# Transformer layer on one core: the next rows turned on VectorE and placed by DMA instead of turned on TensorE

## The chip, the cores and the metric

The kernel runs on one core of one Trainium2 chip. The metric is the device time of one execution in microseconds; lower is better. Before the change three timed runs took 1333.8 to 1335.08 us, with a median of 1334.93.

## The reference

One layer over `x` of 8 sequences x 2048 rows x 256 columns, all in float32:

```python
xn = (x - mean(x)) / sqrt(var(x) + 1e-5)              # layer norm of each row
q, k, v = split(xn @ wqkv); q = relu(q); k = relu(k)  # 16 heads of 16
kv = cumsum(k[..., :, None] * v[..., None, :])        # causal linear attention
attn = (q . kv) / (q . cumsum(k) + 1e-5) @ wo
sc = sigmoid(xn @ Wr); top2 = the two experts of 8 with the largest sc + router_bias
cw = sc at top2, divided by its sum + 1e-9; 0 elsewhere
routed = sum over e < 4 of cw[e] * (silu(xn @ Wg[e]) * (xn @ Wu[e])) @ Wd[e]
routed += (cw[4] + cw[6]) * xn + cw[7] * relu(xn)
shared = causal convolution of xn over 4 rows, per column, + conv_b
out = x + attn + routed + shared
```

Matrix products contract over the columns of `xn`, so TensorE needs `xn` with its columns on the partitions: `xT`. The convolution reads the same `xT`.

## The kernel before

The 16384 rows go in 32 batches of 512, four batches per sequence; `s` is the sequence, `j` the batch in it. A batch is T = 4 tiles of 128 rows. Every operand of a product is split into a high part in TensorE's fast float format and a low part (the rest), and a product is three passes: low x high, high x high, high x low (`product`, L299). For the rows of a batch the high part is `xh` (ScalarE, `high_x`, L530) and the low part `xl` = `xT` - `xh` (GpSimd, `low_x`, L665), each in two halves c = 0, 1 of 128 columns.

Each engine runs its own list of instructions in the order written; semaphores connect them. A batch has on TensorE:
1. for t = 0..3 `gate_up(t)` (expert t, 12 passes of 512 columns for gate, then up) and `numerators(t)` (small attention products of tile t, with the running state, `state_sum`);
2. after the numerators of t = 1, `turn_xn` for the next batch: eight 128 x 128 transposes by the identity into two PSUM banks (L307, called at L489);
3. `heads(s, j, 1)` (L326) for the next batch: values and router scores, then keys and queries. It begins with waits for both halves of `xh` and of `xl` of the next batch;
4. `output(t)` for t = 0..3, with the scores of the next batch ahead of t = 3.

The other engines, in the same batch:
- VectorE, per tile: state blocks (`blocks`), `gate_up` (the product `hid` of up and silu of gate, L836), `attend`, and a tap of the convolution (L828); then the statistics of the batch two ahead, `router`, `key_sums`, `products`, and the output adds, masks and inverses between them.
- ScalarE: silu, high parts, `fill_xT` (L518: copies the three rows of halo and the turned rows from PSUM into `xT`), `high_x` for both halves behind silu(2); then the evictions of `heads`, `same` and `relu` terms.
- GpSimd: `weigh(e)` (multiplies `hid` by the router's weight, L687; waits for VectorE's `hid` of that expert), `low_hid(e)` (L691), `low_y(t)` (L696), in the order weigh 0, low_y 0, weigh 1, low_hid 0, low_y 1, then `low_x` for c = 0 and 1 (L668), weigh 2, low_hid 1, low_y 2, weigh 3, low_hid 2, low_y 3, low_hid 3; then `base` (L671, waits for ScalarE's `same`) and `normalise` (L657, `xn` of the batch two ahead).
- SP: `spread_cw` (the router's weights to DRAM and back, broadcast to all partitions), the store of the batch's output, and the load of the batch four ahead.

`xT`, `xh`, `xl` and `xn` have two buffers each, chosen by the batch's parity.

Of the kernel before, what the change touches and what calls it, by code (L numbers as in the profile page):

```python
# [16 lines left out]
def layer_kernel(nc, x, wqkv, wo, w_router, router_bias, w_gate, w_up, w_down, conv_w, conv_b,  # L17
# [28 lines left out]
    with ExitStack() as ctx:  # L46
# [36 lines left out]
        rstd = sb("rstd", [P, T])  # L83
        xT = sb("xT", [P, 2, C, HALO + BT])
        xh, xl = sb("xh", [P, 2, C, BT], F32R), sb("xl", [P, 2, C, BT], F32R)
# [34 lines left out]
        hh, hl = sb("hh", [P, E, BT], F32R), sb("hl", [P, E, BT], F32R)  # L120
        cT = sb("cT", [P, C, BT])


# [49 lines left out]
        s_halo = sem("s_halo")  # L173
        s_xT = sem("s_xT")
        s_xh = sem("s_xh")
        s_xl = sem("s_xl")
# [47 lines left out]
        def chunk_at(s, j, n):  # L224


            return s * (CHUNKS - 1) + (2 * T * j + n if j < BPS else CHUNKS - 1 + n)

        def load_at(s, jk):

            return s * 16 + (jk // BPS + 1) * 16
# [12 lines left out]
        def _(sp):  # L244
# [15 lines left out]
            def spread_cw(s, j, k):  # L260
# [35 lines left out]
        def _(pe):  # L296
# [93 lines left out]
            def batch(s, j, left):  # L390
# [52 lines left out]
                def output(t):  # L443
# [35 lines left out]
                    else:  # L479
                        turn_conv()  # L480
                        add_attention()
                        add_hidden().then_inc(s_op, 1)

                for t in range(T):
                    gate_up(t)
                    numerators(t)
                    if t == 0:
                        scores(s, j, 0, 1)
                    if t == 1 and not last:  # L489
                        for c in range(C):  # L490
                            turn_xn(s, j, 1, c)
                if not last:
# [17 lines left out]
        def _(act):  # L510
# [6 lines left out]

            def fill_xT(s, j, k):  # L518
                p = (j + k) % 2

                if (j + k) % BPS:
                    act.activation(xT[:, p, :, 0:HALO], xT[:, 1 - p, :, BT:BT + HALO], ACT.Copy).then_inc(s_halo, 1)
                else:
                    act.activation(xT[:, p, :, 0:HALO], zeros[:, 0:C * HALO].rearrange("p (c h) -> p c h", c=C),
                                   ACT.Copy).then_inc(s_halo, 1)
                for c in range(C):
                    act.wait_ge(s_xtr, at(s, j, C, k * C + c + 1))
                    copy(xT[:, p, c, HALO:HALO + BT], XB[c][:, :]).then_inc(s_xT, 1)

            def high_x(s, j, k):  # L530
                p = (j + k) % 2
                for c in range(C):
                    act.wait_ge(s_xT, at(s, j, C, k * C + c + 1))
                    copy(xh[:, p, c, :], xT[:, p, c, HALO:HALO + BT]).then_inc(s_xh, 1)

# [35 lines left out]
            def batch(s, j, left):  # L571
# [16 lines left out]
                def first_tap():  # L588

                    act.wait_ge(s_out, at(s, j, T, T))  # L590
                    act.wait_ge(s_halo, at(s, j, 1, 1))
                    for c in range(C):
                        ins = act.activation(cT[:, c, :], xT[:, j % 2, c, 0:BT], ACT.Identity, bias=conv_bs[:, c:c + 1],
                                             scale=conv_ws[:, c, 0:1])
                    ins.then_inc(s_tap0, 1)
# [29 lines left out]
            for c in range(C):  # L625
# [4 lines left out]
            act.activation(sg[:, 0:1], zeros[:, 0:1], ACT.Sigmoid)  # L630
            act.activation(xT[:, 0, :, 0:HALO], zeros[:, 0:C * HALO].rearrange("p (c h) -> p c h", c=C),
                           ACT.Copy).then_inc(s_halo, 1)
# [15 lines left out]
        def _(pool):  # L648
# [16 lines left out]
            def low_x(s, j, k, c):  # L665
                p = (j + k) % 2
                pool.wait_ge(s_xh, at(s, j, C, k * C + c + 1))
                pool.tensor_tensor(xl[:, p, c, :], xT[:, p, c, HALO:HALO + BT], xh[:, p, c, :].bitcast(F32),  # L668
                                   ALU.subtract).then_inc(s_xl, 1)
# [10 lines left out]
            def batch(s, j, left):  # L680
# [23 lines left out]
                if not last:  # L704
                    for c in range(C):
# [12 lines left out]

# [7 lines left out]
        def _(dve):  # L726
# [24 lines left out]
            def router(s, j, k):  # L751
# [20 lines left out]
                dve.tensor_tensor(c46[:, :], cw[:, E, :], cw[:, E + 2, :], ALU.add).then_inc(s_cw, 1)  # L772

            def key_sums(s, j, k):
                for g in range(C):
# [43 lines left out]
            def batch(s, j, left):  # L819
                last = left == 0  # L820

                def tap(n):
# [4 lines left out]
                    for c in range(C):  # L827
                        ins = dve.scalar_tensor_tensor(out=cT[:, c, :], in0=xT[:, j % 2, c, n:n + BT],  # L828
                                                       scalar=conv_ws[:, c, n:n + 1], in1=cT[:, c, :],
# [69 lines left out]
            for c in (1, 0):  # L899
                dve.wait_ge(s_xtr, C)  # L900
                if c == 0:

                    dve.wait_ge(s_xh, 1)
                ins = dve.tensor_scalar(xT[:, 0, c, HALO:HALO + BT], XB[c][:, :], 1.0, None, ALU.mult)
                ins.then_inc(s_xT, 1)
            for c in range(C):
                dve.wait_ge(s_xT, C)
                dve.wait_ge(s_xh, c + 1)
                dve.tensor_tensor(xl[:, 0, c, :], xT[:, 0, c, HALO:HALO + BT], xh[:, 0, c, :].bitcast(F32),
                                  ALU.subtract).then_inc(s_xl, 1)  # L910
# [62 lines left out]
```

## Time and profile before

| | |
|---|---|
| timed runs | 1333.8, 1334.93, 1335.08 us |
| the profiled execution's own time | 1334.1 us |
| its span, first to last instruction | 1332.3 us |
| TensorE busy (matmul) | 1312.0 us, 98% |
| VectorE busy | 1120.6 us, 84% |
| GpSimd busy | 822.7 us, 62% |
| ScalarE busy | 737.4 us, 55% |
| TensorE's granted clock | 9 tenths or more in all 40 slices of the span, mean 0.997 |
| DMA | 73.73 MB in 46828 packets, mean 55 GB/s |

Busy time is the sum of an engine's instructions, whatever they wait for; it does not tell which engine sets the time. The chain of waits does: it goes back from the last instruction and names at each step what released it. A timeline lists the instructions of one engine in order of time, with the idle time in front of an instruction and what ended it in brackets. Matmuls are pipelined: their listed durations overlap, so what one costs is the distance between starts. Times are in us unless marked ns.

### The profile page before, as it was taken

The page shows a single profiled execution, that of the slowest core. Times are in us where ns is not written, and L with a number is a line of the kernel's source. Part 1 is how long each engine was busy: PE and PEld are TensorE (multiplying, and loading weights), DVE is VectorE, ACT ScalarE, POOL GpSimd, SP SyncE. Part 2 cuts the span into 40 slices and gives each one's busy share as a digit, 9 for nine tenths or more (in the row PEclk, how much of TensorE's full clock was granted, in tenths as well). Part 3 has the DMA queues.
Part 4 walks back from the last instruction along what each step waited for, and adds up shares of the span by engine and source line. Part 5 has one row for each costly group of instructions (what it writes and reads, how often), then busy time and mean ns, then how long its engine had stood idle before and what let it go on. Part 6 is the DMA issues. An engine that isn't in the chain of part 4 may idle for free.

```text
span 1332.3 us, 54753 instructions
## 1 busy us (share of the span) xinstructions
PE 1312.0 (98%) x24384; PEld 1136.9 (85%) x24384; DVE 1120.6 (84%) x2574; ACT 737.4 (55%) x1543; POOL 822.7 (62%) x673
## 2 busy tenths in 40 slices
PE   5999999999999999999999999999999999999998
PEld 4888888888888888888888888888888888888887
DVE  7988889888898888898888988888888889888885
ACT  5645566545556455565555564556645655545561
POOL 2676566675575755666656757556666566575554
PEclk9999999999999999999999999999999999999999
DMA  5011211111211111111111011111111111111110
GB/s 181 30 39 66 66 53 47 35 66 66 66 34 50 51 66 65 50 50 35 66 66 65 35 49 51 66 66 50 50 34 67 66 65 35 35 65 50 51 49 18
DMA packets 46828, 73.73 MB, mean 55 GB/s; under 512 B 6529, under 2 KB 42241, under 8 KB 42497
## 3 DMA queue, kind: packets, MB, share of 16 engines
q1 hardware_dynamic: 45888, 69.23, 15.2%
q8 instruction: 191, 3.13, 1.0%
q10 hardware_dynamic: 704, 1.01, 0.2%
q14 instruction: 45, 0.36, 0.1%
HBM read 53.18 MB, written 17.04 MB: 53 GB/s over the span
## 4 chain that ended last, share of the span: by engine, by line
PE 97%; DVE 1%; POOL 0%; ACT 0%; DMA 0%; issue 0%; POOLq 0%; DVEq 0%
PE ring L303 51%; PE scores L303 17%; PE ring L423 7%; PE ring L439 6%; PE scores L372 5%; PE state_sum L386 4%; PE ring L459 2%; PE scores L312 2%; PE scores L354 2%; DMA x_t<-in_L_attn_x_dram 0%; DVE cT L828 0%; ACT qp L548 0%; DVE sm L807 0%; PE scores L321 0%; POOL hid L687 0%
## 5 line engine op out<-in xcount | busy, mean ns | idle before, releaser
L687 POOL TENSOR_TENSOR hid<-hid,cwb 128x512 f32<-128x512 f32 x128 | 172.0, 1343 | 225.4 <-DVE hid L836 224.7
L828 DVE SCALAR_TENSOR_TENSOR cT<-xT,conv_ws,cT 128x512 f32<-128x512 f32 x192 | 292.3, 1561 | 0.0
L675 POOL TENSOR_TENSOR x_t<-x_t,same 128x1024 f32<-128x1024 f32 x32 | 76.9, 2404 | 242.7 <-ACT same L557 242.7
L814 DVE TENSOR_TENSOR state_bd<-state_sum,tables_s 128x256 f32<-128x256 f32 x248 | 103.7, 418 | 135.9 <-PE state_sum L386 135.8
L578 ACT ACTIVATE sg<-ring 128x512 f32<-128x512 f32 x128 | 76.8, 600 | 251.3 <-PE ring L303 251.3
L303 PE MATMUL ring<-xl,wgu_h 128*128 128x512 f32 x512 | 212.3, 415 | 0.0
L691 POOL TENSOR_TENSOR hl<-hid,hh 128x512 fp32r<-128x512 f32 x128 | 208.4, 1628 | 0.0
L303 PE MATMUL ring<-xh,wgu_l 128*128 128x512 f32 x512 | 203.0, 396 | 0.0
L303 PE MATMUL ring<-xh,wgu_h 128*128 128x512 f32 x512 | 202.2, 395 | 0.0
L511 ACT ACTIVATE yh<-yT 128x256 fp32r<-128x256 f32 x128 | 53.5, 418 | 246.5 <-DVE yT L845 246.5
L807 DVE TENSOR_TENSOR sm<-scores,causal_s 128x512 f32<-128x512 f32 x256 | 158.5, 679 | 21.6 <-PE scores L372 21.6
L303 PE MATMUL ring<-wd_l,hh 128*128 128x256 f32 x512 | 143.5, 280 | 3.4 <-DVE yT L845 2.1
L303 PE MATMUL ring<-wd_h,hl 128*128 128x256 f32 x512 | 143.5, 280 | 0.0
L303 PE MATMUL ring<-wd_h,hh 128*128 128x256 f32 x512 | 143.3, 280 | 0.0
L696 POOL TENSOR_TENSOR yl<-yT,yh 128x256 fp32r<-128x256 f32 x128 | 129.9, 1015 | 0.0
L423 PE MATMUL ring<-sm,vp 64*32 64x64 f32 x8192 | 118.8, 225 | 0.0
L303 PEld LDWEIGHTS ring<-xl,wgu_h 128*128 128x128 f32 x512 | 96.7, 189 | 24.7 <-issue 5.5
L303 PEld LDWEIGHTS ring<-xh,wgu_l 128*128 128x128 f32 x512 | 96.5, 189 | 22.6
L303 PEld LDWEIGHTS ring<-xh,wgu_h 128*128 128x128 f32 x512 | 97.2, 190 | 17.5
L386 PEld LDWEIGHTS state_sum<-vp,ktok 64*32 64x32 f32 x3968 | 54.0, 107 | 55.0 <-issue 49.5
L423 PEld LDWEIGHTS ring<-sm,vp 64*32 64x32 f32 x8192 | 98.1, 105 | 2.9 <-issue 2.9
L303 PE MATMUL scores<-xh,wqk_l 128*128 128x512 f32 x256 | 100.1, 391 | 0.0
(118 smaller groups left out, 3528.1 us busy)
## 6 DMA issues: line engine op xcount, KB each, us to landing
cwb<-cw_rows SPq DMA_DIRECT2D x32, 1024.0 KB, 4.7
x_t<-in_L_attn_x_dram SPq DMA_DIRECT2D x32, 512.0 KB, 4.4
out_dram<-x_t SPq DMA_DIRECT2D x31, 512.0 KB, 2.9
cw_rows<-cwt SPq DMA_DIRECT2D x128, 2.0 KB, 1.4
sm<-in_L_attn_wqkv_dram ACTq DMA_DIRECT2D x2, 384.0 KB, 5.0
sm<-in_L_ffn_Wg_dram SPq DMA_DIRECT2D x2, 256.0 KB, 3.5
sm<-in_L_ffn_Wu_dram SPq DMA_DIRECT2D x2, 256.0 KB, 4.6
cwb<-in_L_ffn_Wd_dram SPq DMA_DIRECT2D x1, 512.0 KB, 5.7
```

Of the source, the lines that this page charges most:

```text
L303: ins = mm(dst, lhs, rhs, start=first and n == 0, stop=final and n == len(passes) - 1, skip_group_check=not (first and final))
L386: ins = mm(ST[rows, g, :], ktok[toks, t, g, rows], vp[toks, t, g * PPG + m, 0:3:2, :], start=first and g == 0, stop=True, skip_group_check ...
L423: mm(NB2[t % 2][h][BLK * m:BLK * m + BLK, gs], window, sm[toks, t // 2, t % 2, 2 * pair + par, :], start=par == 0 and g == 0, stop=False, ...
L439: ins = mm(NB2[t % 2][h][rows, g * HALF:(g + 1) * HALF], state_bd[:, n % 4, cols], qT[:, g, n0:n0 + HALF], start=False, stop=True, skip_gr ...
L578: act.activation(sg[:, :], GB[t % 2], ACT.Silu).then_inc(s_sg, 1)
L675: pool.tensor_tensor(xb, xb, same[:, :, :], ALU.add).then_inc(s_base1, 1)
L687: pool.tensor_tensor(hid[:, e, :], hid[:, e, :], cwb[:, e, :], ALU.mult).then_inc(s_hid, 1)
L691: pool.tensor_tensor(hl[:, e, :], hid[:, e, :], hh[:, e, :].bitcast(F32), ALU.subtract).then_inc(s_hl, 1)
L696: pool.tensor_tensor(yl[:, :, t * P:(t + 1) * P], yT[:, t % 2, :, :], yh[:, :, t * P:(t + 1) * P].bitcast(F32), ALU.subtract).then_inc(s_y ...
L807: dve.tensor_tensor(heads, SB[f][:, :].rearrange("p (t a n) -> p t a n", a=2, n=HALF), causal2_s[:, :].unsqueeze(1).unsqueeze(1).to_broadc ...
L814: dve.tensor_tensor(state_bd[:, n % 4, :].rearrange("p (g m n) -> p g m n", g=C, m=PPG), ST.unsqueeze(2).to_broadcast([P, C, PPG, BLK]), s ...
L828: ins = dve.scalar_tensor_tensor(out=cT[:, c, :], in0=xT[:, j % 2, c, n:n + BT], scalar=conv_ws[:, c, n:n + 1], in1=cT[:, c, :], op0=ALU.m ...
```

## The change

In every batch but the first, `xn` of the batch after next is turned in the output stage of the current batch. VectorE turns it in blocks of 32 x 32 (`turn_x`, four instructions, between `router` and `key_sums`) into a new buffer `xb_t`; SP then issues 32 transfers (`place_turned`), each of which moves one row and one column of blocks of one half to its place in `xT`. TensorE's `turn_xn` stays for batch 1 alone, and so do ScalarE's copies out of PSUM. `normalise` goes ahead of `base` on GpSimd. `high_x` and `low_x` take one half per call, and the second half of each has a new place: on ScalarE behind silu(3), on GpSimd behind `weigh(3)`. `heads` takes over one of the waits of `turn_xn`. In front of `gate_up(0)` of each batch but the last TensorE gets 32 waits for a semaphore that was met at the start. `xT` has 32 columns of lead in place of 3 and another address.

```diff
+    LEAD = 32
+    QUADS = P // 32
+    FILL = 32
+        xT = sb("xT", [P, 2, C, LEAD + BT])
+        xb_t = sb("xb_t", [P, C, QUADS, T, BLK])
+            def place_turned(s, j, k):
+                sp.wait_ge(s_turn, at(s, j, 1, k - 1))
+                for c in range(C):
+                    for a in range(QUADS):
+                        for q in range(QUADS):
+                            row = xT[q * BLK:(q + 1) * BLK, (j + k) % 2, c, LEAD:LEAD + BT]
+                            sp.dma_start(row.rearrange("p (t a n) -> p t a n", t=T, a=QUADS)[:, :, a, :],
+                                         xb_t[a * BLK:(a + 1) * BLK, c, q, :, :]).then_inc(xT_in[c], 16)
...
                 if left:
                     spread_cw(s, j, 1)
+                if left > 1:
+                    place_turned(s, j, 2)
...
             def heads(s, j, k):
                 p = (j + k) % 2
+                if k:
+                    pe.wait_ge(s_sm, at(s, j, U * ROWS, U * ROWS))
                 pe.wait_ge(s_xh, at(s, j, C, k * C + C))
                 pe.wait_ge(s_xl, at(s, j, C, k * C + C))
...
+                if not last:
+                    for _ in range(FILL):
+                        pe.wait_ge(tables_in, 16)
                 for t in range(T):
                     gate_up(t)
                     numerators(t)
                     if t == 0:
                         scores(s, j, 0, 1)
-                    if t == 1 and not last:
+                    if s == j == 0 and t == 1:
                         for c in range(C):
-                            turn_xn(s, j, 1, c)
+                            turn_xn(0, 0, 1, c)
...
                 high_y(1)
                 if not last:
-                    fill_xT(s, j, 1)
+                    lead(s, j, 1)
                 silu(2)
                 if not last:
-                    high_x(s, j, 1)
+                    high_x(s, j, 1, 0)
                 high_hid(1)
                 high_y(2)
                 silu(3)
+                if not last:
+                    high_x(s, j, 1, 1)
...
                 low_y(1)
                 if not last:
-                    for c in range(C):
-                        low_x(s, j, 1, c)
+                    low_x(s, j, 1, 0)
                 weigh(2)
                 low_hid(1)
                 low_y(2)
                 weigh(3)
+                if not last:
+                    low_x(s, j, 1, 1)
                 low_hid(2)
                 low_y(3)
                 low_hid(3)
+                if left > 1:
+                    normalise(s, j, 2)
                 if not last:
                     base(s, j, 1)
-                if left > 1:
-                    normalise(s, j, 2)
...
+            def turn_x(s, j, k):
+                dve.wait_ge(s_xn, at(s, j, 1, k + 1))
+                if s + j:
+                    for c in range(C):
+                        dve.wait_ge(xT_in[c], turned_at(s, j, k - 1))
+                for t in range(T):
+                    ins = dve.transpose(xb_t[:, :, :, t, :], xn[:, (j + k) % 2, t, :]
+                                        .rearrange("p (c q n) -> p c q n", c=C, q=QUADS))
+                ins.then_inc(s_turn, 1)
...
                     router(s, j, 1)
+                    if left > 1:
+                        turn_x(s, j, 2)
                     key_sums(s, j, 1)
```

## Rows read from the trace of the kernel before

**Rows 1.** The chain that ended last, by engine (page, part 4).
```profile
PE 97%; DVE 1%; POOL 0%; ACT 0%; DMA 0%; issue 0%; POOLq 0%; DVEq 0%
```

**Rows 2.** Timeline of TensorE: start, us, line, operation, out<-in, count.
```profile
653.25 1.09 PE L312 MATMUL scores<-tables_s,xn 128*128 128x128 f32 x8
654.10 0.47 PE L303 MATMUL ring<-xl,wgu_h 128*128 128x512 f32 x1
```

**Rows 3.** Timeline of GpSimd in two batches.
```profile
657.09 2.14 POOL L668 TENSOR_TENSOR xl<-xT,xh 128x512 fp32r<-128x512 f32 x2
...
663.41 1.29 POOL L687 TENSOR_TENSOR hid<-hid,cwb 128x512 f32<-128x512 f32 x1
664.66 1.74 POOL L691 TENSOR_TENSOR hl<-hid,hh 128x512 fp32r<-128x512 f32 x1
...
667.50 1.30 POOL L691 TENSOR_TENSOR hl<-hid,hh 128x512 fp32r<-128x512 f32 x1
676.59 2.40 POOL L675 TENSOR_TENSOR x_t<-x_t,same 128x1024 f32<-128x1024 f32 x1 [7.78 <-ACT same L557]
...
745.11 1.29 POOL L687 TENSOR_TENSOR hid<-hid,cwb 128x512 f32<-128x512 f32 x1 [0.42 <-DVE hid L836]
```

**Rows 4.** Timeline of TensorE, first product of `heads` in the same two batches.
```profile
663.22 0.39 PE L303 MATMUL scores<-wvr_l,xh 128*128 128x264 f32 x1
...
744.71 0.39 PE L303 MATMUL scores<-wvr_l,xh 128*128 128x264 f32 x1
```

**Rows 5.** Timeline of VectorE in the first of these batches.
```profile
646.04 0.42 DVE L814 TENSOR_TENSOR state_bd<-state_sum,tables_s 128x256 f32<-128x256 f32 x1 [2.43 <-PE state_sum L386]
...
662.65 0.68 DVE L836 TENSOR_TENSOR hid<-ring,sg 128x512 f32<-128x512 f32 x1
```

**Rows 6.** Timeline of TensorE near the span's start and end, after idle times.
```profile
27.83 1.20 PE L372 MATMUL scores<-qp,kT 32*64 32x128 f32 x64 [2.32 <-ACT ktok L511]
...
30.30 0.63 PE L303 MATMUL ring<-xh,wgu_l 128*128 128x512 f32 x1
30.73 0.63 PE L303 MATMUL ring<-xl,wgu_h 128*128 128x512 f32 x1
...
32.93 0.39 PE L303 MATMUL ring<-xl,wgu_h 128*128 128x512 f32 x1
33.16 0.39 PE L303 MATMUL ring<-xh,wgu_h 128*128 128x512 f32 x1
...
1316.89 0.39 PE L303 MATMUL ring<-wd_l,hh 128*128 128x256 f32 x1 [2.13 <-DVE yT L845]
...
1319.62 0.58 PE L303 MATMUL ring<-wd_l,hh 128*128 128x256 f32 x1 [1.30 <-POOL hl L691]
```

**Rows 7.** Windows: stretch, length, busy by engine, granted clock, DMA share, GB/s.
```profile
29.00:31.00 2.00, 2.00 (x22) 1.65 (x21) 1.97 (x4) 1.55 (x2) 1.65 (x1) 0.52 0.90 369
31.00:33.00 2.00, 2.00 (x7) 1.52 (x7) 2.00 (x4) 0.76 (x3) 0.73 (x1) 0.63 0.26 98
...
1320.00:1322.00 2.00, 2.00 (x11) 2.00 (x11) 0.00 (x0) 0.00 (x0) 0.00 (x0) 0.50 0.00 0
```

**Rows 8.** VectorE groups by shape: busy us, mean ns, idle before in us.
```profile
L789 DVE STREAM_TRANSPOSE qks_tok<-qks 128x512 f32<-128x512 f32 x64 | 41.8, 691 | 1.1
...
L771 DVE STREAM_TRANSPOSE cwt<-cw 128x32 f32<-128x32 f32 x32 | 6.8, 212 | 1.1
...
L764 DVE TENSOR_TENSOR hot<-hot 128x32 f32<-128x32 f32 x32 | 6.3, 197 | 1.1
```

**Rows 9.** Timeline of SP's transfers: start, us to issue, line, out<-in, count.
```profile
672.06 1.71 SPq L265 DMA_DIRECT2D cw_rows<-cwt  x4
674.77 0.34 SPq L272 DMA_DIRECT2D cwb<-cw_rows  x1
```

**Rows 10.** DMA issues (page, part 6): count, KB each, median us to landing.
```profile
cw_rows<-cwt SPq DMA_DIRECT2D x128, 2.0 KB, 1.4
```

**Rows 11.** Timeline of ScalarE, `silu(3)` of the batch after the first of rows 3.
```profile
701.05 0.60 ACT L578 ACTIVATE sg<-ring 128x512 f32<-128x512 f32 x1 [0.70 <-PE ring L303]
```

More of the change, by code:

```diff
@@ L83, in layer_kernel @@
         rstd = sb("rstd", [P, T])
-        xT = sb("xT", [P, 2, C, HALO + BT])
+        xT_gap = sb("xT_gap", [P, 12])
         xh, xl = sb("xh", [P, 2, C, BT], F32R), sb("xl", [P, 2, C, BT], F32R)
@@ L121, in layer_kernel @@
         cT = sb("cT", [P, C, BT])
+        xT_room = sb("xT_room", [P, 8])
+        xT = sb("xT", [P, 2, C, LEAD + BT])
+        xb_t = sb("xb_t", [P, C, QUADS, T, BLK])
         rdT = qks
@@ L174, in layer_kernel @@
         s_xT = sem("s_xT")
+        s_turn = sem("s_turn")
+        xT_in = [sem(f"xT_in{c}") for c in range(C)]
         s_xh = sem("s_xh")
@@ L227, in chunk_at, with turned_at @@
             return s * (CHUNKS - 1) + (2 * T * j + n if j < BPS else CHUNKS - 1 + n)
+        def turned_at(s, j, k):
+            return (s * BPS + j + k - 1) * (16 * QUADS * QUADS)
         def load_at(s, jk):
@@ L516, in high_weights, with lead, high_x @@
                     copy(hi, src).then_inc(w_hi, 1)
-            def fill_xT(s, j, k):
+            def lead(s, j, k):
                 p = (j + k) % 2
                 if (j + k) % BPS:
-                    act.activation(xT[:, p, :, 0:HALO], xT[:, 1 - p, :, BT:BT + HALO], ACT.Copy).then_inc(s_halo, 1)
+                    act.activation(xT[:, p, :, LEAD - HALO:LEAD], xT[:, 1 - p, :, LEAD + BT - HALO:LEAD + BT],
+                                   ACT.Copy).then_inc(s_halo, 1)
                 else:
-                    act.activation(xT[:, p, :, 0:HALO], zeros[:, 0:C * HALO].rearrange("p (c h) -> p c h", c=C),
+                    act.activation(xT[:, p, :, LEAD - HALO:LEAD], zeros[:, 0:C * HALO].rearrange("p (c h) -> p c h", c=C),
                                    ACT.Copy).then_inc(s_halo, 1)
-                for c in range(C):
-                    act.wait_ge(s_xtr, at(s, j, C, k * C + c + 1))
-                    copy(xT[:, p, c, HALO:HALO + BT], XB[c][:, :]).then_inc(s_xT, 1)
-            def high_x(s, j, k):
-                p = (j + k) % 2
-                for c in range(C):
-                    act.wait_ge(s_xT, at(s, j, C, k * C + c + 1))
-                    copy(xh[:, p, c, :], xT[:, p, c, HALO:HALO + BT]).then_inc(s_xh, 1)
+                if s + j == 0:
+                    for c in range(C):
+                        act.wait_ge(s_xtr, C + c + 1)
+                        copy(xT[:, p, c, LEAD:LEAD + BT], XB[c][:, :]).then_inc(s_xT, 1)
+            def high_x(s, j, k, c):
+                p = (j + k) % 2
+                if s + j:
+                    act.wait_ge(xT_in[c], turned_at(s, j, k))
+                else:
+                    act.wait_ge(s_xT, C + c + 1)
+                copy(xh[:, p, c, :], xT[:, p, c, LEAD:LEAD + BT]).then_inc(s_xh, 1)
             def heads(s, j, k):
@@ L592, in first_tap @@
                     for c in range(C):
-                        ins = act.activation(cT[:, c, :], xT[:, j % 2, c, 0:BT], ACT.Identity, bias=conv_bs[:, c:c + 1],
+                        ins = act.activation(cT[:, c, :], xT[:, j % 2, c, LEAD - HALO:LEAD - HALO + BT], ACT.Identity, bias=conv_bs[:, c:c + 1],
                                              scale=conv_ws[:, c, 0:1])
@@ L630, in _ @@
             act.activation(sg[:, 0:1], zeros[:, 0:1], ACT.Sigmoid)
-            act.activation(xT[:, 0, :, 0:HALO], zeros[:, 0:C * HALO].rearrange("p (c h) -> p c h", c=C),
+            act.activation(xT[:, 0, :, LEAD - HALO:LEAD], zeros[:, 0:C * HALO].rearrange("p (c h) -> p c h", c=C),
                            ACT.Copy).then_inc(s_halo, 1)
@@ L667, in low_x @@
                 pool.wait_ge(s_xh, at(s, j, C, k * C + c + 1))
-                pool.tensor_tensor(xl[:, p, c, :], xT[:, p, c, HALO:HALO + BT], xh[:, p, c, :].bitcast(F32),
+                pool.tensor_tensor(xl[:, p, c, :], xT[:, p, c, LEAD:LEAD + BT], xh[:, p, c, :].bitcast(F32),
                                    ALU.subtract).then_inc(s_xl, 1)
@@ L704, in batch @@
                 if not last:
-                    for c in range(C):
-                        low_x(s, j, 1, c)
+                    low_x(s, j, 1, 0)
                 weigh(2)
@@ L772, in router @@
                 dve.tensor_tensor(c46[:, :], cw[:, E, :], cw[:, E + 2, :], ALU.add).then_inc(s_cw, 1)
+            def turn_x(s, j, k):
+                dve.wait_ge(s_xn, at(s, j, 1, k + 1))
+                if s + j:
+                    for c in range(C):
+                        dve.wait_ge(xT_in[c], turned_at(s, j, k - 1))
[3 more added lines that the diff above has]
+                ins.then_inc(s_turn, 1)
             def key_sums(s, j, k):
@@ L827, in tap @@
                     for c in range(C):
-                        ins = dve.scalar_tensor_tensor(out=cT[:, c, :], in0=xT[:, j % 2, c, n:n + BT],
+                        ins = dve.scalar_tensor_tensor(out=cT[:, c, :], in0=xT[:, j % 2, c, LEAD - HALO + n:LEAD - HALO + n + BT],
                                                        scalar=conv_ws[:, c, n:n + 1], in1=cT[:, c, :],
@@ L903, in _ @@
                     dve.wait_ge(s_xh, 1)
-                ins = dve.tensor_scalar(xT[:, 0, c, HALO:HALO + BT], XB[c][:, :], 1.0, None, ALU.mult)
+                ins = dve.tensor_scalar(xT[:, 0, c, LEAD:LEAD + BT], XB[c][:, :], 1.0, None, ALU.mult)
                 ins.then_inc(s_xT, 1)
@@ L908, in _ @@
                 dve.wait_ge(s_xh, c + 1)
-                dve.tensor_tensor(xl[:, 0, c, :], xT[:, 0, c, HALO:HALO + BT], xh[:, 0, c, :].bitcast(F32),
+                dve.tensor_tensor(xl[:, 0, c, :], xT[:, 0, c, LEAD:LEAD + BT], xh[:, 0, c, :].bitcast(F32),
                                   ALU.subtract).then_inc(s_xl, 1)
```

## Prediction

> **What bounds the kernel now.** I read the chain of waits first: TensorE holds 97% of it [rows 1], so TensorE's own work sets the time, and another engine counts only where TensorE has to wait for it. The span of 1332.3 us holds 32 batches of one pattern, some 41 us each, so a stage can be read from one batch. Then I read the timeline of each engine over that batch, looking for two things: what TensorE no longer does, and which wait would now end last in front of it.
>
> **The transposes that go.** Eight transposes start at 653.25 and the next product at 654.10 [rows 2], so they cost TensorE 0.85 us. They stand in every batch but the last, 31 times, and the change keeps them in the first, so 30 x 0.85 = 25.5 us come off. With them go ScalarE's two copies out of PSUM per batch; ScalarE is busy for 55% of the span, so these give nothing.
>
> **The wait that comes.** The diff also moves work that its title does not name. Before, both halves of the low part (`low_x`, c = 0 and 1) ran on GpSimd ahead of `weigh(2)`: they start at 657.09 and take 2.14 us [rows 3], and TensorE's `heads` starts at 663.22 [rows 4], four microseconds later. After, `low_x(1)` stands behind `weigh(3)` in GpSimd's queue. `weigh(3)` waits for `hid` of tile 3, which VectorE makes from the last gate and up product; and `heads` waits for both halves in its first lines, before it does anything. So a chain VectorE `hid` - GpSimd `weigh(3)` - GpSimd `low_x(1)` - TensorE `heads` is formed, and on TensorE only `numerators(3)` lies beside it.
>
> Its length, against the moment at which `heads` could start (663.22 and 744.71 in two batches [rows 4]):
> - VectorE's `hid` of tile 3 starts at 662.65 and takes 0.68 [rows 5], so it ends 0.11 after that moment, and `weigh(3)` follows at 663.41, 0.19 after it; in the other batch `weigh(3)` starts at 745.11 [rows 3], 0.40 after it. I take 0.2 (0 to 0.4), the nearer of the two, since GpSimd has one operation less before it. The 0.85 us does not shorten this: VectorE, which waits for TensorE's state sum in every tile, moves up with TensorE.
> - `weigh(3)` holds GpSimd from 663.41 to 664.66 [rows 3]: 1.25.
> - `low_x(1)`: 1.07 each in the pair of before. Here it runs beside VectorE's convolution taps, where `hl`, an operation of the same shape, takes 1.74 instead of 1.30 [rows 3]. 1.07 x 1.74 / 1.30 = 1.43 (1.07 to 1.74).
> - GpSimd's end to TensorE's first product: 0.15 (0.05 to 0.2), as an estimate from the 0.08 between the end of VectorE's `hid` and `weigh(3)` and a first weight load that is no longer done ahead.
>
> Sum 0.2 + 1.25 + 1.43 + 0.15 = 3.0 us of an idle TensorE in each of 31 batches (2.4 to 3.5): 93 us. It does not come back: before, TensorE had nothing to wait for that this idle time could hide.
>
> **The clock.** TensorE stood for 2.32 us before 27.83, and for 2.13 and 1.30 us before 1316.89 and 1319.62 [rows 6]. After the first of these the granted clock reads 0.52 and 0.63, after the others 0.50 [rows 7]: the lower level, 1.2 GHz instead of 2.4, for some 3.4 us each time. At that level a product of 512 columns comes every 0.43 us (30.30 to 30.73), at the upper level every 0.23 (32.93 to 33.16) [rows 6]. Eight fit in 3.4 us, so a low stretch costs 8 x 0.20 = 1.6 us; I take 1.55, because the narrower products of `heads` lose a little less. Both places in the running kernel where TensorE stood over 2 us were followed by one, and a gap of 3 us is longer than either. I take 28 of 31: 28 x 1.55 = 43 us (0 to 48).
>
> **What is added on VectorE.** Four 32 by 32 block transposes of 128 x 256, between `router` and `key_sums`. The trace has them at 128 x 32 (212 ns) and 128 x 512 (691 ns) [rows 8]; four cost 0.85 to 2.8 us, by their place between the two about 1.5. Behind them on VectorE wait key sums, products, output adds and masks, for which TensorE waits at the start of the next batch. There VectorE sits idle for 2.43 us, waiting for TensorE [rows 5]; with the new wait in front of `heads` it also gets to `router` before its scores are there. So nothing; without that cover it would be up to 31 x 2.8 = 87 us. `normalise` is moved ahead of `base` on GpSimd, which stands idle there for 7.78 us until ScalarE delivers `same` [rows 3], so into that idle time; should the transposes have to wait a little for it, the same 2.43 us cover that.
>
> **What is added on SP.** 32 transfers per batch, behind the spread of the router's weights and ahead of the output store. Four small ones take 1.71 us to issue [rows 9], 0.43 each: 13.7 us from about 675.1 (674.77 + 0.34 [rows 9]), and a small one lands 1.4 us later [rows 10], so all lie by 690. The second half is wanted after `silu(3)` of the next batch, 701.05 + 0.5 [rows 11]. That leaves over 11 us, so nothing; the store and the next load go out some 5 us later, with more than a batch to spare. This holds until a transfer takes over 0.78 us ((701.55 - 675.1 - 1.4) / 32).
>
> The transfers move runs of 128 bytes. The Trainium skill (DMA: Bandwidth & Descriptors, Specifications) says that below 512 bytes the engines do a read-modify-write; its section on why small descriptors are slow limits the penalty to HBM. By the second the sum stays as it is; by the first the landing grows, and only past the 0.78 us does time move. No row shows 4096 such runs in one batch.
>
> **The 32 waits in front of `gate_up`.** All have long been met. A wait that VectorE puts between two of its operations leaves it idle for 1.1 us in 32 times, 34 ns each [rows 8], the time of the signal included. So 32 cost at most 1.1 us a batch, 34 us in all; below nothing is excluded, since they do no work. Nothing if TensorE's queue holds enough work: the output products just ahead take 1.4 us per tile. I take nothing. The Trainium skill (TensorE: Matmul & The Clock Gate, on engine queue depths) gives TensorE a queue of 64; by it the sum has 0 here, by the row alone up to 34 us more.
>
> **The sum.** On the profiled execution (1334.1 us, span 1332.3; the three timed runs have a median of 1334.93, 0.06% above): 1334.1 - 25.5 + 93 + 43 = 1444.6 us, say 1445: slower by 8%.
>
> **Rivals.**
> 1. *The stall without the clock.* The gap falls so that the clock stays up. For it: in the running batches the granted clock was never low. Against it: [rows 6, 7]. 1334.1 - 25.5 + 93 = 1402 us.
> 2. *The chain is hidden; faster.* `low_x(1)` is done before `numerators(3)` ends, TensorE keeps its 0.85 us. For it: GpSimd is busy 62% of the span only, and the data comes a batch ahead. Against it: `weigh(3)` alone ends 1.4 us after `heads` is due [rows 3, 4]. It decides where the stall is under 0.82 us a batch (25.5 / 31); without any, 1334.1 - 25.5 = 1309 us.
> 3. *The transfers come late.* Their runs are short and there are 4096 of them in a batch. If each transfer took 1 us, 675.1 + 32 + 1.4 = 708.5 against 701.55 would add 7 us in each of 30 batches: 1445 + 210 = 1655 us. Against it: the room of 11 us.
> 4. *The 32 waits are in the open*: 1445 + 34 = 1479 us.
>
> **How the numbers follow.** Forecast 0.63, its own range 1420 to 1465 (28 falls, 2.4 to 3.5 us of stall give 1427 to 1460). Rival 1 0.23 (1384 to 1418), rival 2 0.06, rival 3 0.04, rival 4 0.04. The range 1388 to 1472 holds the forecast and nearly all of rival 1. Faster by over 0.2% needs rival 2: 0.05; within 0.2% (what a measurement of this kernel can tell from no change) its edge, where the stall just eats the gain: 0.01; slower 0.94.
>
> **What would show it.** TensorE idle in front of the first product of `heads` for about 3 us, 31 times, released by GpSimd's `xl`; `xl` of c = 1 starting right behind `weigh(3)`; the granted clock at 0.5 for a few microseconds in most batches, TensorE's busy share near 92%; no transposes of `xn` but the first; block transposes of some 0.43 us; `place_turned` over before the output store; no idle time in front of `gate_up(0)`. The prediction is wrong if `heads` starts without a gap, and 43 us too high if the clock stays up.

## The result, and the profile after

The changed kernel takes 1476.26 us (1471.71 to 1479.86 in four runs) where the kernel before takes 1334.91: ratio 1.1058, 95% interval 1.1045 to 1.1071. It was forecast at 1445 in a range up to 1472. The direction and the chain of causes came as forecast; the sum was 31 us too small, and the time lies above the top of the stated range. The profiled execution takes 1474.79 us, with a span of 1473.0 and a mean granted clock of 0.955 (0.997 before).

The page of the changed kernel, parts 1 and 4 (it answers to [rows 1]):

```profile
PE 1342.3 (91%) x24144; PEld 1164.6 (79%) x24144; DVE 1215.5 (83%) x2694; ACT 715.3 (49%) x1483; POOL 827.9 (56%) x673
...
PE 81%; DVE 10%; POOL 7%; issue 2%; ACT 0%; DMA 0%; POOLq 0%; DVEq 0%
```

VectorE and GpSimd, which had 1% of the chain between them, now have 17%. The view of waits of TensorE (who waits for whom; us in total, times, longest) says where:

```profile
PE scores L330 <- POOL xl L710: 102.9, 31, 3.4
...
PE scores L402 <- issue: 5.4, 7, 0.9
...
PE ring L330 <- issue: 2.1, 2, 1.4
```

One large new wait, 31 times, 3.32 us each: the first product of `heads` waits for GpSimd's `low_x`. The chain that ended last shows one of these gaps piece by piece (start, us, what):

```profile
726.80 0.69 DVE hid L891
727.49 0.07 issue
727.55 1.27 POOL hid L729
728.82 1.68 POOL xl L710
730.50 0.14 issue
730.63 2.98 PE scores L330 x12
```

This is VectorE `hid` - GpSimd `weigh(3)` - GpSimd `low_x(1)` - TensorE `heads`. On GpSimd's own timeline the two halves of `low_x` were back to back in [rows 3]; here they stand apart, and the second one is longer:

```profile
722.10 1.28 POOL L710 TENSOR_TENSOR xl<-xT,xh 128x512 fp32r<-128x512 f32 x1
...
728.77 1.71 POOL L710 TENSOR_TENSOR xl<-xT,xh 128x512 fp32r<-128x512 f32 x1
```

TensorE over the same stretch (it answers to [rows 2], [rows 4] and [rows 6]):

```profile
717.65 0.69 PE L469 MATMUL ring<-qT,state_bd 128*64 128x64 f32 x16
718.26 0.50 PE L330 MATMUL ring<-xl,wgu_h 128*128 128x512 f32 x1
...
726.75 0.69 PE L469 MATMUL ring<-qT,state_bd 128*64 128x64 f32 x16
730.63 0.56 PE L330 MATMUL scores<-wvr_l,xh 128*128 128x264 f32 x1 [3.20 <-POOL xl L710]
730.99 0.42 PE L330 MATMUL scores<-wvr_h,xh 128*128 128x264 f32 x1
731.21 0.42 PE L330 MATMUL scores<-wvr_h,xl 128*128 128x264 f32 x1
...
736.05 0.63 PE L330 MATMUL scores<-xl,wqk_h 128*128 128x512 f32 x1
736.48 0.54 PE L330 MATMUL scores<-xh,wqk_h 128*128 128x512 f32 x1
736.86 0.40 PE L330 MATMUL scores<-xh,wqk_l 128*128 128x512 f32 x1
737.09 0.39 PE L330 MATMUL scores<-xl,wqk_h 128*128 128x512 f32 x1
...
741.63 0.39 PE L330 MATMUL scores<-xh,wqk_l 128*128 128x512 f32 x1
```

The kernel before has, ahead of the transposes of [rows 2] and at the end of the `heads` of [rows 4]:

```profile
652.64 0.69 PE L439 MATMUL ring<-qT,state_bd 128*64 128x64 f32 x16
...
671.48 0.39 PE L303 MATMUL scores<-xh,wqk_l 128*128 128x512 f32 x1
```

Behind the gap a product of 264 columns starts every 0.22 us, where the trace of the kernel before has 0.12, and the 512-column products come 0.43 apart until 736.48, then 0.23 (736.86 to 737.09): the lower clock level lasts some 6 us of this `heads`. From its first to its last product it takes 11.00 us (730.63 to 741.63), before the change 8.26 (663.22 to 671.48). The windows say it directly (stretch, length, busy us by engine with counts for TensorE, weight load, VectorE, ScalarE, GpSimd, then granted clock, DMA share, GB/s; it answers to [rows 7]):

```profile
728.00:731.40 3.40, 0.77 (x3) 0.80 (x4) 3.40 (x4) 0.99 (x2) 3.40 (x3) 0.79 0.22 71
732.00:735.40 3.40, 3.40 (x18) 3.40 (x17) 2.06 (x9) 2.62 (x7) 3.19 (x5) 0.50 0.00 0
736.00:739.40 3.40, 3.40 (x16) 2.81 (x15) 2.34 (x21) 1.11 (x4) 1.50 (x3) 0.88 0.00 0
```

This batch is one of the slower ones. Windows of 12 us, each from about the start of a gap, show three kinds of batches:

```profile
189.00:201.00 12.00, 8.84 (x58) 7.71 (x55) 11.11 (x44) 6.45 (x16) 10.02 (x11) 1.00 0.01 4
592.00:604.00 12.00, 8.64 (x69) 7.89 (x56) 9.92 (x38) 5.14 (x13) 10.37 (x11) 0.86 0.15 45
727.00:739.00 12.00, 8.80 (x52) 8.18 (x48) 9.05 (x34) 4.74 (x12) 10.20 (x11) 0.72 0.14 43
```

Of the 31 gaps, 2 read 1.00 (the clock did not fall), 22 read 0.86 and 7 read 0.72. Since the lower level is half the upper one, 0.86 means some 3.4 us of 12 at the lower level, and 0.72 twice that. The `heads` behind them take 8.24 us, 9.70 and 10.92 in the mean. Summed over the 31 batches they take 306.2 us, against 256.4 before the change: 49.9 us more.

VectorE's idle time and new transposes, and SP's transfers (answering to [rows 5, 8, 9]):

```profile
736.77 0.22 DVE L797 TENSOR_TENSOR scoreb<-score,bias_s 128x32 f32<-128x32 f32 x1 [2.64 <-ACT score L580]
...
739.90 1.42 DVE L825 STREAM_TRANSPOSE xb_t<-xn 128x256 f32<-128x256 f32 x4
```

```profile
698.96 22.82 SPq L297 DMA_DIRECT2D xT<-xb_t  x32
```

The transposes cost what was estimated (411 ns each in the mean over 120). The placing takes 0.71 us a transfer in this batch, not 0.43, and still ends in time: no wait of ScalarE for it stands in this trace.

In front of `gate_up(0)` the changed kernel has idle time once, in the first batch:

```profile
30.63 0.77 PE L330 MATMUL ring<-xl,wgu_h 128*128 128x512 f32 x1 [1.44 <-issue]
```

**The sum of the parts.** 1332.3 - 25.5 (transposes) + 102.9 (the gap) + 49.9 (`heads` behind it, the clock) + 7.5 (idle on "issue", none of it before) = 1467.1, for a span of 1473.0. The 5.9 us that are left are busy time of TensorE outside these `heads`: 1342.3, against 1312.0 - 25.5 + 49.9 = 1336.4. Their cause stays open. As much stands in experiments 7 and 10, where the clock stays up behind the gaps.

### The profile page after: what moved, and what is told of

Read it like the earlier page. It is cut to its first block, busy times and chain, and to the rows that moved or that the text cites. A ratio compares the mean times of both kernels' runs of the same rounds, so it can differ in the third digit from the quotient of the medians.

```text
span 1473.0 us, 55758 instructions
## 1 busy us (share of the span) xinstructions
PE 1342.3 (91%) x24144; PEld 1164.6 (79%) x24144; DVE 1215.5 (83%) x2694; ACT 715.3 (49%) x1483; POOL 827.9 (56%) x673
## 4 chain that ended last, share of the span: by engine, by line
PE 81%; DVE 10%; POOL 7%; issue 2%; ACT 0%; DMA 0%; POOLq 0%; DVEq 0%
PE ring L330 42%; PE scores L330 18%; DVE cT L883 6%; PE scores L402 5%; PE ring L453 5%; PE ring L469 4%; POOL xl L710 4%; PE state_sum L416 3%; POOL hid L729 3%; PE ring L489 2%; PE scores L384 2%; DVE hid L891 1%; DVE yT L900 1%; DVE state_bd L869 1%; DMA x_t<-in_L_attn_x_dram 0%
## 5 line engine op out<-in xcount | busy, mean ns | idle before, releaser
L729 POOL TENSOR_TENSOR hid<-hid,cwb 128x512 f32<-128x512 f32 x128 | 164.0, 1281 | 339.8 <-DVE hid L891 339.0
L883 DVE SCALAR_TENSOR_TENSOR cT<-xT,conv_ws,cT 128x512 f32<-128x512 f32 x192 | 302.5, 1614 | 0.0
L330 PE MATMUL scores<-wvr_l,xh 128*128 128x264 f32 x128 | 53.2, 416 | 105.7 <-POOL xl L710 102.9
L330 PEld LDWEIGHTS scores<-wvr_l,xh 128*128 128x128 f32 x128 | 36.2, 283 | 109.4 <-issue 109.4
L738 POOL TENSOR_TENSOR yl<-yT,yh 128x256 fp32r<-128x256 f32 x128 | 122.3, 956 | 0.0
L330 PEld LDWEIGHTS ring<-xh,wgu_l 128*128 128x128 f32 x512 | 96.5, 188 | 22.8 <-issue 0.2
L330 PE MATMUL scores<-xl,wqk_h 128*128 128x512 f32 x256 | 101.9, 398 | 0.0
```

Of the source, the lines that this page charges most:

```text
L330: ins = mm(dst, lhs, rhs, start=first and n == 0, stop=final and n == len(passes) - 1, skip_group_check=not (first and final))
L729: pool.tensor_tensor(hid[:, e, :], hid[:, e, :], cwb[:, e, :], ALU.mult).then_inc(s_hid, 1)
L738: pool.tensor_tensor(yl[:, :, t * P:(t + 1) * P], yT[:, t % 2, :, :], yh[:, :, t * P:(t + 1) * P].bitcast(F32), ALU.subtract).then_inc(s_y ...
```

## The experiments

All times are medians, each set against runs of the kernel before on the same chip (1334.1 to 1335.5). Where an experiment stands on another, its diff is against that one.

**1. The order undone, the change kept.** Both halves of the next batch are split and subtracted together again, ahead of `weigh(2)`.

```diff
 # ScalarE
                     high_x(s, j, 1, 0)
+                    high_x(s, j, 1, 1)
...
                 silu(3)
-                if not last:
-                    high_x(s, j, 1, 1)
 # GpSimd
                     low_x(s, j, 1, 0)
+                    low_x(s, j, 1, 1)
                 weigh(2)
...
                 weigh(3)
-                if not last:
-                    low_x(s, j, 1, 1)
```

> The change with the second halves back where they stood: high_x(1) right behind high_x(0), low_x(1) right behind low_x(0), both ahead of weigh(2). Theory A (the loss is the wait of heads for low_x(1), 3.3 us in 31 batches, and the low clock that follows it): both go, the 25.5 us of the transposes stay off, so 1305 to 1320 us, no idle time of TensorE in front of heads, mean granted clock back at 0.99 or more. Theory B (the loss is the added work: the short transfers, VectorE's transposes, the 32 waits): little changes, 1440 to 1480 us.

Measured: 1517.06 us, 1.1374 [1.1355, 1.1393]; both theories missed it. The wait of `heads` is gone, as theory A said, but another took its place, and it is larger:

```profile
PE ring L489 <- DVE x_t L938: 128.5, 30, 4.4
```

The timelines of VectorE, GpSimd and TensorE show why:

```profile
713.03 1.42 DVE L823 STREAM_TRANSPOSE xb_t<-xn 128x256 f32<-128x256 f32 x4
...
716.83 5.47 DVE L839 TENSOR_TENSOR qks<-qT,ksum 128x512 f32<-128x512 f32 x2
...
724.87 0.74 DVE L938 TENSOR_TENSOR x_t<-ring,x_t 128x256 f32<-128x256 f32 x2
...
716.38 2.61 POOL L716 TENSOR_TENSOR x_t<-x_t,same 128x1024 f32<-128x1024 f32 x1 [3.38 <-ACT same L597]
719.07 2.68 POOL L719 TENSOR_TENSOR x_t<-x_t,xn 128x1024 f32<-128x1024 f32 x1
...
725.34 0.69 PE L489 MATMUL ring<-tables_s,cT 128*128 128x128 f32 x2 [4.40 <-DVE x_t L938]
```

VectorE's two `products` (two SBUF inputs) take 5.47 us instead of 1.29. The first is due at 716.83, when GpSimd's `base` has run since 716.38; the pair ends at 722.30, 0.55 behind the end of `base` (721.75). Before, the pair ended at 675.60 and `base` began at 676.59 [rows 3]. The new transposes push the products back by 1.4 us, and a tiny operation beside GpSimd's `hl`, `vare`, takes another 1.1 (1.29 for 0.16 before). The first output add waits behind them, and TensorE for that. In the changed kernel the two do not meet: there the pair is over at 744.87, and `base` begins at 746.73, when ScalarE's `same` is done. That it is the gap which holds `same` back so long was not tried by itself.

**2. The order alone, without the change.** The kernel before, with only the second half moved as the change moves it (`high_x` takes the half as an argument here, too; that edit is left out below).

```diff
-                    high_x(s, j, 1)
+                    high_x(s, j, 1, 0)
 # ScalarE, behind silu(3)
+                if not last:
+                    high_x(s, j, 1, 1)
 # GpSimd
-                    for c in range(C):
-                        low_x(s, j, 1, c)
+                    low_x(s, j, 1, 0)
 # GpSimd, behind weigh(3)
+                if not last:
+                    low_x(s, j, 1, 1)
```

> The kernel before with one part of the change alone: the second halves moved, high_x(1) behind silu(3), low_x(1) behind weigh(3); the transposes stay on TensorE, nothing is added on SP or VectorE. Theory A: 1335 + 31 x 3.3 + some 57 for the clock = 1495 us (1480 to 1505), slower than the whole change by its 25.5 us less what the change adds elsewhere. Theory B: 1335 us, as before.

Measured: 1477.96 us, 1.1071 [1.1053, 1.1090]: the whole loss, with the transposes still on TensorE and no new transfer, and 2 us below the range of theory A, since the gaps are 2.82 us each and not 3.3.

```profile
PE scores L303 <- POOL xl L670: 87.4, 31, 3.0
```

1332.3 + 87.4 + 60.0 (TensorE's busy time, 1372.0 against 1312.0) = 1479.7, for a span of 1479.4. All 31 gaps are followed by a low stretch. No idle time on "issue" stands in this trace.

**3. TensorE kept busy in the gap.** The changed kernel with 13 products into a buffer that `heads` overwrites, ahead of its two waits.

```diff
 # TensorE, heads, ahead of its waits for the split halves
+                    for _ in range(13):
+                        mm(SB[0][:, :], wqk_h[:, 0, 0:P], xh[:, 1 - p, 0, :], start=True, stop=True)
```

> The change with 13 products of 512 columns put in front of the two waits at the head of heads, into a PSUM bank that is free there and is written over afterwards; they fill about 3.0 of the 3.3 us in which TensorE stands. They leave the stall as long as it is. Theory A: the clock stays at its upper level and its share comes off, some 57 us of 1476: 1410 to 1430 us, mean granted clock 0.99. If the clock were no part of the loss: 1476 us or a little more.

Measured: 1436.89 us, 1.0770 [1.0752, 1.0788], clock 0.995: 39 us faster for 403 products of work that nobody needs.

```profile
PE scores L404 <- issue: 13.5, 16, 1.4
...
PE scores L330 <- POOL xl L712: 5.8, 23, 0.3
```

The 31 `heads` take 255.3 us again, for 306.2 in the changed kernel. So the clock's term is a consequence of the gap. It missed the expected 1410 to 1430 by 7 us; the idles on "issue" doubled (13.5 + 1.6 = 15.1 against 7.5).

**4. Without the 32 met waits** in front of `gate_up` (`FILL = 0`).

```diff
-    FILL = 32
+    FILL = 0
```

> The change without the 32 met waits in front of gate_up(0). Theory A: they cost nothing, 1470 to 1480 us. If they are in the open at up to 34 ns each: 31 x 1.1 = 34 us come off, 1442 us.

Measured: 1478.11 us (1471.65 to 1481.09), against the change's 1471.71 to 1479.86: no difference that these runs can tell. One place does differ. The first `gate_up(0)`, which in the changed kernel starts behind 1.44 us of idle time, starts here without any:

```profile
29.98 0.79 PE L330 MATMUL ring<-xl,wgu_h 128*128 128x512 f32 x1
```

**5. The collision taken out.** Experiment 1, with `base` of the next batch held until the denominators are summed.

```diff
             def base(s, j, k):
+                if k:
+                    pool.wait_ge(s_den, at(s, j, 1, k + 1))
```

> This is the early order (both halves of the next batch split before the second weighting) with one wait more: GpSimd's 'base' of the next batch waits until VectorE's denominators are summed. Theory A (the 128.5 us in which TensorE waited for the first output add came from one collision: VectorE's two-input product, 0.69 us apart from GpSimd and 2.6 us beside GpSimd's two-input 'base'): the mean of the product falls from 2623 ns to 0.7, the wait of L489 for x_t from 128.5 us to under 30 (the add then ends about 0.3 us behind TensorE: 30 x 0.3 = 9), the clock goes above 0.98, and the time is 1315 to 1340. Theory B (VectorE's chain is late by the transposes themselves, 1.3 us, and by the statistics' 1.1 us, base or not): products still 0.7 us but a wait of over 1 us in each batch, and the time 1380 to 1480. If the placing on SP (22.8 us, ended at 739) is now late, ScalarE shows a wait for it before the split, under 4 us in each batch.

Measured: 1401.67 us, 1.0505 [1.0488, 1.0523], 115 us faster than experiment 1. The products are back at their old time, and TensorE's wait for the add is 0.7 us in all (group of VectorE: busy, mean ns):

```profile
L841 DVE TENSOR_TENSOR qks<-qT,ksum 128x512 f32<-128x512 f32 x64 | 41.4, 688 | 1.1
```

The collision was the cause of that wait. The time is still not that of theory A: with TensorE faster the placing comes late, as the last sentence of the expectation allowed for.

```profile
ACT xh L547 <- DMA xT<-xb_t: 123.9, 30, 6.8
```

```profile
PE state_sum L416 <- ACT sg L618: 30.1, 20, 3.5
```

ScalarE stands 4.1 us a batch in front of the second half, a little over the 4 that were allowed for, and its silu behind that is late for TensorE.

**6. The same without the 32 waits** (`FILL = 0`).

> The run before without the 32 met waits in front of the turned batch's products. Theory A (the met waits cost nothing even where TensorE is not held up by anything else): the same time within 3 us. Theory B (they were hidden only by the stall): 5 to 34 us faster.

Measured: 1404.45 us (1400.63 to 1406.89) against 1397.6 to 1405.22: no difference, here too. The 1.44 us ahead of the first `gate_up(0)` stand in experiment 5 and are gone in this one.

**7. The second half one place later.** Experiment 5, with the split behind `silu(3)` and the subtraction between `low_y(2)` and `weigh(3)`.

```diff
 # ScalarE
-                    high_x(s, j, 1, 1)
...
                 silu(3)
+                if not last:
+                    high_x(s, j, 1, 1)
 # GpSimd
-                    low_x(s, j, 1, 1)
...
                 low_y(2)
+                if not last:
+                    low_x(s, j, 1, 1)
                 weigh(3)
```

> As the first of these, but the second half is split behind the last silu and subtracted between GpSimd's third low_y and its last weighting, so that the placing has some 5 us more. Theory A (only what stands on GpSimd between the half's turn and heads counts, and here nothing does): the same as the first within 10 us, and no wait for the placing. Theory B (the subtraction, 1.3 to 1.7 us, now delays the last weighting and so TensorE's last sums): a wait of 0.5 to 1.5 us in each batch at ring for hl or hid, 15 to 60 us more than the first with its clock.

Measured: 1361.55 us, 1.0201 [1.0184, 1.0218]. The placing is in time again, but `low_x(1)` delays `weigh(3)`, ends 1.2 us after `heads` is due, and a smaller gap is back, 1.27 us each; the clock stays up (0.995).

```profile
PE scores L330 <- POOL xl L710: 39.5, 31, 1.6
```

Neither theory had it whole: the wait is B's in size, but it stands at `heads`, not at the sums.

**8. The transposes behind the first two output adds.** Experiment 7, with VectorE's `turn_x` moved.

```diff
-                    if left > 1:
-                        turn_x(s, j, 2)
                     key_sums(s, j, 1)
...
                 for t in range(T):
+                    if t == 2 and left > 1:
+                        turn_x(s, j, 2)
```

> As the third of these, but VectorE turns the rows behind its first two output adds, not ahead of the key sums: the four transposes are then off the chain products, denominators, first add. Theory A (that chain is what the transposes were in the way of): the wait of L489 for x_t goes to nearly nothing, the placing starts some 4 us later and is still there for the second half; time 1305 to 1320. Theory B (the place on VectorE does not matter once base is held back): the same as the third within 3 us. Theory C (the placing now comes late for the first half): ScalarE waits at the split and the time goes up by 20 us or more.

Measured: 1498.00 us, 1.1217 [1.1199, 1.1236]: theory C. SP's placing starts 5 us behind the weights' rows and runs into the split.

```profile
710.93 0.34 SPq L287 DMA_DIRECT2D cwb<-cw_rows  x1
716.25 24.42 SPq L297 DMA_DIRECT2D xT<-xb_t  x32
```

```profile
ACT xh L547 <- DMA xT<-xb_t: 122.4, 30, 5.3
```

```profile
PE scores L330 <- POOL xl L710: 119.1, 31, 5.1
```

**9. Two queues for the placing.** Experiment 5, with two transfers ahead of the wait for the weights' rows and the last four on ScalarE's queue, behind the denominators. The lines below are the main ones; `place` issues the transfers from one number up to another.

```diff
+        EARLY, SPLIT = 2, 28
 # SP, behind the four transfers of the weights' rows
+                    place(sp, s, j, 2, 0, EARLY)
 # SP, place_turned: 26 of the 32
+                place(sp, s, j, k, EARLY, SPLIT)
 # ScalarE, behind denominators
+                    place(act, s, j, 2, SPLIT, 32)
```

> The early order with base held back, in which ScalarE waited 123.9 us in all (30 times, about 4.1) for the placing, which took SP 23.8 us. Here two of the 32 transfers go out while the weights' rows are still on their way, and the last four from ScalarE's queue behind the denominators; everything else is the same. Theory A (the whole loss left, 66 us, is the late placing: 6 x 0.72 = 4.3 us sooner leaves nothing of it): ScalarE's wait for the placing under 20 us, no wait of TensorE for sg, and 1310 to 1330. Theory B (the transfers cost what their descriptors cost, on whichever queue: the queue is not the limit, or ScalarE's own issues hold its silu up by 2.9 us): the placing still ends after 22 us or the silu is late, and the time is within 15 us of 1401.

Measured: 1336.67 us (1331.76 to 1346.87), 1.0024 [1.0003, 1.0045]: 65 us faster than experiment 5 and level with the kernel before. ScalarE's wait for the placing is 13.2 us in all (123.9 there), TensorE's wait for `sg` 0.3. Theory A named the cause; its 1310 to 1330 missed by 7 us.

**10. The second half once more later.** Experiment 9, split behind `high_y(2)`, subtracted behind `low_hid(1)`.

```diff
 # ScalarE
                 high_y(2)
+                if not last:
+                    high_x(s, j, 1, 1)
 # GpSimd
                 low_hid(1)
+                if not last:
+                    low_x(s, j, 1, 1)
                 low_y(2)
```

> As the one before, but the second half is split behind ScalarE's third high_y and subtracted behind GpSimd's second low_hid, still ahead of the last weighting by one low_y: a few us more for the placing. Theory A: nothing waits for the placing any more, the half is subtracted before the last weighting, so heads does not wait either: 1308 to 1325, faster than before by 1 to 2%. Theory B (GpSimd has no room for 1.3 to 1.7 us anywhere in the last 20 us ahead of heads): heads waits 1 us or more in each batch as when the subtraction stood one step later (39.5 us), and the time is 1350 to 1365.

Measured: 1339.35 us, 1.0035 [1.0021, 1.0049], between the ranges of both theories. `heads` waits again, 0.6 us each:

```profile
PE scores L336 <- POOL xl L718: 17.9, 30, 0.7
```

**11. That subtraction one step up**, ahead of `low_hid(1)`.

```diff
+                if not last:
+                    low_x(s, j, 1, 1)
                 low_hid(1)
-                if not last:
-                    low_x(s, j, 1, 1)
```

> As the one before, in which the second half's subtraction ended 0.5 us too late for heads (17.9 us in all), but with that subtraction one step up on GpSimd, behind its third weighting and ahead of its second low_hid (1.7 us sooner); nothing else. Theory A (the 17.9 us and the idles they bring are all that is left of the loss): no wait of TensorE for xl, and 1312 to 1325, 1 to 1.5% faster than before. Theory B (GpSimd's work as a whole is what is late, and the wait only moves to the sums that low_hid feeds): a wait for hl of some 0.5 us in each batch, 1330 to 1345. Theory C (something that no named wait shows, as the idles on issue and the tenth of a batch that differs between runs of the two-queue kernels): no named wait and still 1328 to 1340.

Measured: 1336.22 us (1333.61 to 1341.54), 1.0022 [1.0010, 1.0034]: theory C. No wait of TensorE for `xl` is left, and no gain:

```profile
PE ring L495 <- DVE x_t L950: 4.7, 22, 0.2
...
PE scores L408 <- issue: 5.3, 4, 1.6
...
PE ring L336 <- issue: 2.7, 3, 1.4
...
PE state_sum L422 <- DVE x_t L950: 1.1, 7, 0.2
```

Its span, 1334.4, is 1332.3 - 25.5 + 17.3 more idle time of TensorE + 10.3 more busy time. Of the 17.3, 8.0 are on "issue" and 5.8 wait for the output add, a fifth of a microsecond at a time; the rest is smaller still. Of the 10.3 a part is the clock (0.995 against 0.997); the rest stays open, and with it why 25.5 us less of transposes leave no gain.

## Why the prediction fell short

**What is missing.** On the profiled execution the sum said 1444.6, and 1474.8 came. The 30.2 us are 9.9 of the gap, 6.9 of the clock, 7.5 of idle time on "issue" and 5.9 of other busy time. All four lie on the same side.

**The transposes that go: right.** With them the next `gate_up` starts 1.46 us behind the product in front of them (652.64 to 654.10), without them 0.61 (717.65 to 718.26): 0.85 us, 30 times. TensorE's busy time does not fall by all of it. In experiments 7 and 10, where the clock stays up, it is 1292.3 and 1292.1, 20 us below the 1312.0 of before and not 25.5.

**The wait that comes: right in mechanism, 10 us too small; the largest miss.** It was forecast as 0.2 + 1.25 + 1.43 + 0.15 = 3.0 us. The chain shown above reads 0.12 (from the end of TensorE's work, 727.43, to 727.55) + 1.27 + 1.68 + 0.13; in the mean of the 31 batches the four terms are 0.24 + 1.22 + 1.71 + 0.15 = 3.32. The term that was mis-sized is `low_x(1)`: 1.71 us, for which the forecast took 1.43. It scaled the time of the old place, 1.07, by what the taps do to `hl`. Its own upper row, 1.74, was of an operation of the same shape at the very place where this one was moved, beside VectorE's taps; that row would have been the price. Experiment 2 shows that the order alone makes the gap, and experiment 1 that it goes with the order.

**The clock: right that it falls, 7 us too small.** The step that failed is "for some 3.4 us each time", taken as the length of every low stretch. The clock fell behind 29 of the 31 gaps, where the forecast took 28, and a low stretch of that length cost `heads` 1.43 us, where it took 1.55. But 7 of the 29 lasted twice as long and cost 2.65 us each. Together that is 49.9 us for 43. The few low stretches of before, all at its ends, were no sample of what follows a gap in the running kernel; the upper end of the forecast's bound, 48 us, fell with the same assumption. The prediction's "both places" left one out, too: in the kernel before TensorE also stood for 2.80 us ahead of 13.67, and the granted clock from 13.00 to 20.00 is 1.00.

**Idle time on "issue": not foreseen, 7.5 us.** 1.4 us of it belong to the 32 waits (see below). The rest, 3 to 14 us, stands in every kernel that has the placing and in neither kernel that lacks it (before, and experiment 2). That the many short transfers cause it is argued from this alone and was not tried by itself.

**VectorE's transposes at nothing: right only behind the gap.** The prediction named a cover, an idle 2.43 us at the batch's start, and 87 us without it. Experiment 1 shows what lay without it: 128.5 us, more than the bound, since the cost is not the transposes' length but what they push VectorE's products into. The Trainium skill (SBUF — State Buffer, Who interferes with whom) says that a VectorE instruction with two SBUF inputs contends with a GpSimd instruction that reads SBUF, and that such contention is an exclusive lock. Experiments 1 and 5 agree (2623 ns a product beside `base`, 688 away from it; the pair ended just behind `base`). The prediction did not weigh it in this step.

**SP's placing at nothing: right, with less room than thought.** 0.71 us a transfer (22.82 / 32) lies just under the 0.78 that the prediction gave as its limit; the placing took 22.8 us, not 13.7. As soon as TensorE is faster it is the next wait: 123.9 us of ScalarE in experiment 5, nearly all gone in 9, where two transfers go out early and four on a second queue. A transfer lands 1.9 us later (median), for 1.4 of the small ones in [rows 10]. The Trainium skill (DMA: Bandwidth & Descriptors, Specifications) has a read-modify-write below 512 bytes, which the prediction weighed: both numbers went up, but no run here tells what the length of the runs did from what their number and the size of the transfers did.

**The 32 waits at nothing: right**, with the gap (experiment 4) and without it (6). By the row alone it could have been 34 us. The one exception is the first batch: there TensorE had no work left ahead of them, and they left it idle for 1.44 us, 45 ns each.

**The rivals.** Rival 1 fell with the clock's windows and experiment 3. Rival 2 put the change without its gap at 1309; the best that the runs came to is 1336, since the products beside `base` and then the placing come up one behind the other as soon as TensorE no longer stands, and what holds the last 27 us is open. Rivals 3 and 4 did not come.

## What to carry to other kernels

Read the order that a diff changes before the operation it is named for: here one subtraction (with the split that feeds it), moved behind a multiplication that waits for VectorE, cost 143 us (experiment 2), and what the new way of transposing costs came to light only when that order was undone (experiment 1). Price an operation by the row of its neighbour at its new place, not by its own row at the old one, and add the clock's loss to a gap of TensorE that comes back in every batch, with a range for its length. "Hidden behind a wait" is true for as long as the wait lasts: when it goes, look for the next in line, on every engine and queue, before counting a gain.

## What the runs showed of the hardware

- A two-input operation of VectorE on 128 x 512 took 2623 ns in the mean beside GpSimd's two-input 128 x 1024, and 688 away from it (experiments 1 and 5). `vare`, 128 x 4, went from 162 ns to 1189 in the changed kernel, where it runs beside GpSimd's `hl`.
- Behind gaps of TensorE of 3.32 us in the mean the granted clock fell in 29 of 31 batches, behind gaps of 2.82 us in all 31 (experiment 2), behind gaps of 1.27 us in none (experiment 7, where `heads` took 255.5 us in all, for 256.4 before).
- Filling an idle TensorE with 403 useless products took 39 us off the time (experiment 3).
- A transfer of 16 KB in runs of 128 bytes took SP 0.73 us to issue in the mean of the changed kernel's 960. Four of them on ScalarE's queue took 3.55 us in one batch of experiment 9 (680.12 to 683.67; 2.5 to 4.0 over all), in which ScalarE began nothing else.
- 32 waits that had long been met left TensorE idle for 1.44 us where it had no work left ahead of them (first batch; gone without them in experiments 4 and 6), and for none that the runs can tell in the other batches.
